# Query and key projections folded into one matrix, with a re-ordered software pipeline, in a two-block transformer kernel

## The reference

```
h = _layernorm(x, ln1_g, ln1_b) * (1.0 + g1) + be1
Q = h @ Wq + bq
K = h @ Wk + bk
V = h @ Wv + bv
scores = jnp.einsum('bsd,btd->bst', Q, K) / jnp.sqrt(jnp.float32(dim))
attn = jax.nn.softmax(scores, axis=-1) @ V
x = x + a1 * attn
```

## Time and profile before

| | |
|---|---|
| median of 3 runs | 791.42 us (789.38 to 791.88) |
| the profiled execution | 789.95 us |
| its span, first to last instruction | 788.1 us |
| mean granted TensorE clock | 0.912 of 2.4 GHz |
| set-up, to the first step | about 134 us |
| steps from one q_mm to the next, 273.8 to 632.5 us | 10 in 358.7 us, 35.87 us each |
| drain behind the last q_mm | 632.5 to 788.1 us |

### The profile page before, as it was taken

The page is one execution under the profiler, slowest core; times in us unless marked ns, Lnnn a source line. Parts: engine busy times, 40 slices in busy tenths (PEclk is TensorE's granted clock), DMA queues, the critical chain, the costliest instruction groups (busy, mean ns, idle before and its releaser), DMA issues.

```text
span 788.1 us, 13091 instructions
## 1 busy us (share of the span) xinstructions
PE 628.5 (80%) x3560; PEld 487.7 (62%) x3588; DVE 620.6 (79%) x1432; ACT 568.3 (72%) x1206; POOL 458.3 (58%) x647
## 2 busy tenths in 40 slices
PE   0631336899899999999999999999999998874552
PEld 0110212678777878888787878788888877642321
DVE  3779888223768999999899989998899889888653
ACT  1234670447689999898989999998989888774431
POOL 2203360213647686867767686867678586856623
PEclk9955579799999999999999999999999999985866
DMA  8495800111010101202021011112021010110100
GB/s 312 150 408 204 297 0 25 30 38 47 1 68 35 46 37 48 68 15 68 13 67 47 33 47 47 37 43 66 14 67 34 22 40 22 49 34 1 34 14 14
DMA packets 17821, 51.96 MB, mean 66 GB/s; under 512 B 2880, under 2 KB 3712, under 8 KB 16880
## 3 DMA queue, kind: packets, MB, share of 16 engines
q1 hardware_dynamic: 17488, 50.92, 18.7%
q10 hardware_dynamic: 288, 0.52, 0.2%
HBM read 47.10 MB, written 4.33 MB: 65 GB/s over the span
## 4 chain that ended last, share of the span: by engine, by line
PE 58%; DVE 20%; issue 9%; POOL 5%; ACT 5%; DMA 2%; SPq 1%; DVEq 0%; POOLq 0%; ACTq 0%
PE bank L1346 15%; PE bank L1401 14%; PE bank L1339 7%; PE bank L1474 6%; PE bank L1326 5%; PE bank L1392 5%; DVE qa_dx L872 4%; PE bank L1318 2%; PE bank L1524 2%; PE bank L1489 2%; DVE arena L1138 2%; DVE qa_am L860 2%; DMA arena<-wo_dram 1%; POOL arena L512 1%; DVE arena L1009 1%
## 5 line engine op out<-in xcount | busy, mean ns | idle before, releaser
L1392 PE MATMUL bank<-arena,w 128*128 128x256 f32 x512 | 117.8, 379 | 0.0
L1401 PE MATMUL bank<-arena,w 128*128 128x256 f32 x512 | 116.7, 381 | 1.0 <-ACT arena L633 1.0
L1392 PEld LDWEIGHTS bank<-arena,w 128*128 128x128 f32 x512 | 96.1, 190 | 15.0
L1401 PEld LDWEIGHTS bank<-arena,w 128*128 128x128 f32 x512 | 94.9, 190 | 13.0 <-ACT arena L633 1.2
L1326 PE MATMUL bank<-ident,arena 128*128 128x128 f32 x448 | 66.9, 283 | 21.8 <-ACT arena L685 16.1
L1474 PE MATMUL bank<-tern_wm,qTm 128*128 128x512 bf16 x228 | 71.5, 403 | 15.1 <-ACT arena L707 6.2
L512 POOL TENSOR_TENSOR arena<-arena,row_nm 128x1024 f32<-128x1024 f32 x32 | 75.4, 2357 | 6.6 <-ACT junk_u L715 6.6
L1326 PEld LDWEIGHTS bank<-ident,arena 128*128 128x128 f32 x448 | 53.1, 145 | 35.1 <-issue 20.1
L694 ACT ACTIVATE arena<-arena,round_col,qa_qs 128x256 f32<-128x256 f32 x96 | 50.5, 592 | 22.4 <-DVE qa_qs L881 22.4
L1346 PE MATMUL bank<-arena 128*128 128x256 f32 x256 | 61.5, 383 | 3.1 <-DVE arena L899 3.1
L827 DVE BATCH_NORM_STATS2 ln_st<-arena 128x6 f32<-128x256 f32 x128 | 48.0, 417 | 18.1 <-POOL arena L502 11.7
(11 more groups left out here) (212 smaller groups left out, 1729.2 us busy)
## 6 DMA issues: line engine op xcount, KB each, us to landing
arena<-rows_d SPq DMA_DIRECT2D x32, 384.0 KB, 3.8
...
```

What stands on the lines that cost most here:

```text
L1392: last = te.matmul(bank[3 - q % 2][:, m * S:(m + 1) * S], w1[:, k, (2 * q + m) * P:(2 * q + m + 1) * P], h2T[:, k, :], start=k == 0, stop= ...
L1401: last = te.matmul(bank[3][:, c * S:(c + 1) * S], w2[:, k, c * P:(c + 1) * P], g[:, k, :], start=k == 0, stop=k == HC - 1)
```

## The change

On the chip, once, `query_key` computes `Wqk = Wq Wk^T` (bank 3), and the columns `Wk bq`, `Wq bk` and the number `bq.bk` (bank 0); ACT copies them out. Since `Q K^T = (h Wqk + Wk bq) h^T + (h Wq bk + bq.bk)`, with the last term constant along a row, `q_mm` multiplies by `Wqk`, its bias is `Wk bq`, and `s_mm` multiplies by `hT` in place of `kT`. `k_mm` and `kT` are gone. The row term is kept: `q_mm` ends with 4 matmuls of one column each (`hT` stationary, 128x128, `Wq bk` moving), the part `d` on DVE makes `dots`, and `score_max` computes `top = max/16 + dots` and `nbias = dots - top`. `s_mm` waits for `d`. The list of parts has 136 entries in a new order. The scratch for dynamic DMA is given as 1024 and six small tiles are added.

```diff
 SCHEDULE = [
...
+    ("vv", 5), ("q_mm", 2), ("sq_so", 5), ("xn2T", 3), ("gates1", 6), ("silu0", 6), ("qT", 2), ("so_rstd", 5),
+    ("load_rows1", 3), ("sq_o", 5), ("silu1", 6), ("s_mm", 2), ("ln3_rstd", 4), ("h2T", 3), ("sq_a", 4), ("z_o", 5),
+    ("val1", 6), ("load_rows2", 5), ("gates2", 6), ("up0", 3), ("o_rstd", 5), ("gates3", 6), ("load_x", 0),
+    ("silu2", 6), ("val2", 6), ("z_i", 4), ("sq_u0", 6), ("silu3", 6), ("g0", 3), ("d", 2), ("a_rstd", 4), ("g1", 3),
+    ("mx_a", 4), ("u0", 6), ("sq_u1", 6), ("mx_b", 4), ("am_o", 5), ("u1", 6), ("g2", 3), ("qTo_mm", 5),
+    ("quant_o", 5), ("round_i", 4), ("round_f", 4), ("am_i", 4), ("u2", 6), ("int_o", 5), ("am_f", 4), ("up1", 3),
+    ("z_f", 4), ("val3", 6), ("u3", 6), ("g3", 3), ("gate_o", 5), ("yo", 5), ("am_g", 4), ("scales_ifg", 4),
+    ("up2", 3), ("exp", 2), ("score_max", 2), ("up3", 3), ("z_g", 4), ("store", 6), ("int_i", 4), ("xb", 2),
+    ("z_u0", 6), ("v_mm", 2), ("ln4_moments", 5), ("load_rows0", 0), ("qT_i", 4), ("round_g", 4), ("sq_m", 5),
+    ("ln1_norm", 1), ("x4", 5), ("z_u1", 6), ("qT_f", 4), ("v", 2), ("down0", 3), ("probT_mm", 2), ("my_a", 5),
+    ("si", 4), ("yi", 4), ("qT_g", 4), ("int_g", 4), ("int_f", 4), ("ln4_rstd", 5), ("u_rstd", 6), ("my_b", 5),
...
+    ("hT", 1), ("ln2_rstd", 2), ("x5", 6), ("val0", 5), ("gate_u", 6), ("ln2_norm", 2), ("x3", 3), ("ob", 4),
+    ("ln3_moments", 3), ("back", 3), ("gates0", 5)]
...
-            for w, n in ((wq, "Wq"), (wk, "Wk"), (wv, "Wv")):
+            for w, n in ((wqT, "WqT"), (wkT, "WkT"), (wv, "Wv")):
...
             def evac_q(b):
-                wait(act, s["q_mm"], b)
+                wait(act, s["q_mm"], b, 1, 2)
                 wait(act, s["s_mm"], b.back(1))
                 for c in range(C):
-                    last = sc.activation(qT[:, c, :], bank[1][:, c * S:(c + 1) * S], ACT.Identity, bias=bq[:, c:c + 1])
+                    last = sc.activation(qT[:, c, :], bank[1][:, c * S:(c + 1) * S], ACT.Identity, bias=wk_bq[:, c:c + 1])
...
+            act.wait_ge(s["qk_mm"], 1)
+            sc.activation(wk_bq[:, :], bank[0][:, 0:C], ACT.Copy)
+            sc.activation(wq_bk[:, :], bank[0][:, C:2 * C], ACT.Copy)
+            sc.activation(bq_bk[:, :], bank[0][:, 2 * C:2 * C + 1], ACT.Copy).then_inc(s["qk_sb"], 1)
+            act.wait_ge(s["qk_mm"], 2)
+            sc.activation(flat(wqk[:, :, :]), bank[3][:, :], ACT.Copy).then_inc(s["qk_sb"], 1)
             act.wait_ge(s["cond_steps"], 10)
             act.wait_ge(s["feat_loaded"], 80)
             parts["ln1_norm"](Batch(0, 0))
...
-            def evac_k(b):
-                wait(dve, s["k_mm"], b)
-                wait(dve, s["s_mm"], b.back(1))
-                for c in range(C):
-                    last = ve.tensor_scalar(kT[:, c, :], bank[0][:, c * S:(c + 1) * S], bk[:, c:c + 1], None, ALU.add)
-                last.then_inc(s["kT_ready"], 1)
+            def row_dots(b):
+
+                wait(dve, s["q_mm"], b, 2, 2)
+                ve.tensor_scalar(dots[:, :], bank[0][:, 0:T], bq_bk[:, 0:1], D ** -0.5, ALU.add, ALU.mult).then_inc(s["d_ready"], 1)
...
-                wait(dve, s["smax_ready"], b)
-                ve.tensor_scalar(nbias[:, :], smax[:, :], -(D ** -0.5), None, ALU.mult).then_inc(s["nbias_ready"], 1)
+                wait(dve, s["smax_ready"], b, 1, 3)
+                ve.scalar_tensor_tensor(out=top[:, :], in0=smax[:, :], scalar=D ** -0.5, in1=dots[:, :], op0=ALU.mult,
+                                        op1=ALU.add).then_inc(s["smax_ready"], 1)
+                wait(dve, s["smax_ready"], b, 2, 3)
+                ve.tensor_tensor(nbias[:, :], dots[:, :], top[:, :], ALU.subtract).then_inc(s["smax_ready"], 1)
...
-                feature_major(1, wq, hT, s["q_mm"])
-
-            def k_mm(b):
-                wait(pe, s["hT_ready"], b)
-                feature_major(0, wk, hT, s["k_mm"])
+                feature_major(1, wqk, hT, s["q_mm"])
+                for j in range(T):
+                    for k in range(C):
+                        last = te.matmul(bank[0][:, j:j + 1], hT[:, k, j * P:(j + 1) * P], wq_bk[:, k:k + 1],
+                                         start=k == 0, stop=k == C - 1)
+                last.then_inc(s["q_mm"], 1)
...
             def s_mm(b):
                 wait(pe, s["qT_ready"], b)
-                wait(pe, s["kT_ready"], b)
-                token_major(0, qT, kT, C, s["s_mm"])
+                wait(pe, s["d_ready"], b)
+                token_major(0, qT, hT, C, s["s_mm"])
...
+            def query_key():
+
+                for c, w, x in ((0, wkT, bq), (C, wqT, bk)):
+                    for m_ in range(C):
+                        for k in range(C):
+                            te.matmul(bank[0][:, c + m_:c + m_ + 1], w[:, k, m_ * P:(m_ + 1) * P], x[:, k:k + 1],
+                                      start=k == 0, stop=k == C - 1)
+                for k in range(C):
+                    last = te.matmul(bank[0][:, 2 * C:2 * C + 1], bq[:, k:k + 1].broadcast_to([P, P]), bk[:, k:k + 1],
+                                     start=k == 0, stop=k == C - 1)
+                last.then_inc(s["qk_mm"], 1)
+                for m_ in range(C):
+                    for k in range(C):
+                        last = te.matmul(bank[3][:, m_ * D:(m_ + 1) * D], wqT[:, k, m_ * P:(m_ + 1) * P], wkT[:, k, :],
+                                         start=k == 0, stop=k == C - 1)
+                last.then_inc(s["qk_mm"], 1)
...
-                    for n_ in ("xn1T", "q_mm", "k_mm"):
-                        parts[n_](Batch(0, 0))
+                    pe.wait_ge(s["feat_loaded"], 80)
+                    pe.wait_ge(s["ada_x"], 5)
+                    query_key()
+                    pe.wait_ge(s["qk_sb"], 1)
+                    parts["xn1T"](Batch(0, 0))
+                    pe.wait_ge(s["qk_sb"], 2)
+                    parts["q_mm"](Batch(0, 0))
```

More of the change, by code:

```diff
@@ L6 @@
 SCHEDULE = [
-    ("mx_a", 4), ("so_rstd", 5), ("sq_so", 5), ("q_mm", 2), ("vv", 5), ("k_mm", 2), ("u0", 6), ("silu0", 6),
-    ("qT", 2), ("sq_o", 5), ("ln3_rstd", 4), ("z_o", 5), ("silu1", 6), ("gates1", 6), ("kT", 2), ("mx_b", 4),
-    ("o_rstd", 5), ("z_i", 4), ("am_o", 5), ("u1", 6), ("xn2T", 3), ("quant_o", 5), ("val1", 6), ("a_rstd", 4),
-    ("h2T", 3), ("gates2", 6), ("u2", 6), ("z_f", 4), ("am_i", 4), ("int_o", 5), ("u3", 6), ("am_f", 4), ("am_g", 4),
[4 rows of a table removed]
-    ("v_mm", 2), ("load_x", 0), ("v", 2), ("u_rstd", 6), ("qT_f", 4), ("z_m", 5), ("down0", 3), ("qT_g", 4),
```

40 lines of the change are left out of this document (24 added, 16 removed), and 11 rows, old and new, of the table SCHEDULE.

## The result

| | before | after |
|---|---|---|
| median on the same chip | 790.40 us (789.02 to 791.88) | 807.32 us (805.43 to 808.06) |
| ratio | | 1.0213, 95% interval 1.0188 to 1.0239 |
| span of the profiled execution | 788.1 us | 805.3 us |
| mean granted clock | 0.912 | 0.893 of 2.4 GHz |

What follows compares the result with a forecast made beforehand. PE was taken as the nearly full bound, with DVE and ACT close behind. Steps 3 to 5 (3.6 us) plus steps 6 to 17 (2.4) less set-up (1.3) took 4.7 off 789.95: 785.2, or 786.5 on the median, range 773 to 800.

Steps and rivals of the forecast that it cites:

- PE saves 0.86 us a step: On PE, dropping k_mm saves 1.73 us a step and the eight column instructions add 0.87.
- The columns are dear: Rival, chance 0.22: q_mm's eight column loads take 1.5 to 2.0 us and delay d; 796 to 803 us, taken as 798.
- d, s_mm's waits and top cost nothing: On DVE and PE, s_mm's two waits are covered, and top, held to 17.8 us, ends before exp at 19.6.
- qa_dx ends with z_u0, qa_dq is held by x4: On DVE beside POOL, qa_dx ends with z_u0; qa_dq takes 1.2 us or more and ends with x4.
- The port is free: Rival, chance 0.27: x4 doesn't hold qa_dq, down0 starts at 17.2 us, the step takes 34.6, the kernel 774.
- z_u0 ends at 14.1, since ob stands ahead of back: POOL's chain starts 0.44 us earlier behind ob, so z_u0 ends at 14.1 us into the step instead of 14.54.
- The rest takes 16.98 + 0.25: From down0 to the step's end: 16.98 us as before, plus 0.25 because yg waits for int_g on ACT.
- Set-up +1.3: Before the loop, four more copies on ACT ahead of ln1_norm add 1.3 us; query_key fits in PE's idle time.
- The drain: 0, +-3: The last steps, which have no k_mm, were left at nothing, +-3 us, since their order changed too.
- The order doesn't fit on ACT: Rival, chance 0.09: 0.2 to 0.5 us more waiting at exp, si or sq_m eats each step's gain; 789 to 793 us.

Runs made afterwards that it cites:

- norow_new: Changed kernel without the one-column products, dots and top, nbias being minus the scaled maximum; 802.85 us, ratio 1.0168.
- gate_late_rows: Changed kernel with gate_o behind score_max, and load_rows1 right behind load_rows2 on SP's queue; 800.12 us, ratio 1.013.
- mx_first: Changed kernel with mx_a ahead of vv on VectorE; 802.60 us, ratio 1.0179.
- drain_old: Changed kernel with the order of the kernel before in the last steps alone, from step 16 on; 795.44 us, ratio 1.0082.
- plain_new: Kernel before, unfolded, in the new order, with k_mm behind q_mm and kT in d's place; 814.91 us, ratio 1.0331.
- best3_fold: Changed kernel with mx_a before vv, gate_o behind score_max, old last steps, ln1_norm before sq_m, ln1_moments before ln4_moments, SP loads reordered; 851.63 us, ratio 1.0807.

## Why the prediction was wrong

For the profiled execution the forecast was 785.2 us and 807.1 came. Of the 21.9 us between, 11.5 lie behind the last q_mm, 9.0 in the loop, 0.9 in the set-up and 0.3 in steps 3 to 5. The steps of the forecast, in its own order:

- *PE saves 0.86 us a step.* The columns: 0.81 for eight, foreseen 0.87. Right. Steps 3 to 5, where PE alone sets the pace, gave 3.25 us of the foreseen 3.6. "The columns are dear" is out: in norow_new their removal gave 0.22 us a step.
- *d, s_mm's waits and top cost nothing.* Right in the loop: s_mm stands without a wait before it, top is held 1.60 us and ends before exp is due, and the whole row term, columns and all, is worth 0.22 us.
- *qa_dx ends with z_u0, qa_dq is held by x4.* Right, 1.19 or 1.20 us in twelve of the sixteen batches, 0.17 in the first two and 2.26 in the last two. "The port is free" is out. But the rival's sum for a step without the hold, 34.6 us, isn't right either: with qa_dq free and x4 late (gate_late_rows) the step did not shorten.
- *z_u0 ends at 14.1, since ob stands ahead of back.* **This step failed, twice.** GpSimd's chain doesn't start with sq_so: so_rstd stands behind x5 on its queue and starts at T+0.8 in both kernels, so ob's place gave nothing (mx_first: z_u0 ends at T+14.7, before 14.7). And mx_a behind vv runs into z_o, and z_u0 ends 0.3 us later for it; mx_first gives that back in this step, and 0.13 us a step on the mean. The 14.54 that the forecast started from is itself 0.16 too small: it counts from 417.33, where the chain has q_mm, and the first record is at 417.17. I had used the hold for the one instruction that I was looking at, and not looked for others that the new order puts beside GpSimd's large additions.
- *The rest takes 16.98 + 0.25.* It took 17.40 in this step, where the same stretch of the kernel before takes 17.15 from record to record (453.27 less 436.12; 16.98 has the chain's 0.17 in it). So the 0.25 came, but by luck: not at yg, before which PE never waited in the ten steps, but before the transposes of qTm, where PE waits for int_u3 (L1064), which the new order puts behind x2. On the mean of ten steps the rest is 0.36 longer. This and the 0.8 us of down0 make the 36.5 us against 35.7.
- *Set-up +1.3.* +2.2 in this execution. ACT's four copies took 0.75 us and not 1.3, but between them ACT waited 0.95 us for the product of the weights; the first q_mm, s_mm and the products ran at 0.50 of the clock, 1.2 GHz. The eleven other kernels with the same set-up had the q_mm of step 3 between 142.6 and 144.6 us, so a part of it is scatter.
- *The drain: 0, +-3.* **The term that failed most**: +11.5, and drain_old gives 10.7 of it back; plain_new has the same loss without the fold. I had left it at nothing because I hadn't worked it out. What hardly counts in the loop counts here: moving gate_o (gate_late_rows) takes 6.4 us off this part, moving mx_a (mx_first) 2.7. Behind PE's gaps the clock is at 1.2 GHz for longer, which alone adds 2.5 us to down0.
- *The order doesn't fit on ACT* (the third rival) did not show in the changed kernel, where PE never waited for int_g; it did in gate_late_rows, 1.0 us a step.

What stays open is the exact source of the loop's 0.6 us. Each of three waits was taken away in turn (for round_i, for qT_g's eviction, and, by mx_a's place, for z_i) and the step stayed between 36.3 and 37.1: in this order several chains over the three other engines end within some tenths of a microsecond of each other, and PE is late by the longest that is left. The old order has room where the new one has none: there ln1_moments fills the time in which x4 waits. That this is the whole of the 0.6 us is argued, not shown; best3_fold, which was to show it, tested something else.
